# Retention and the product-key stage in one block: hoisted set-up, the second layer norm taken pair by pair, and the first similarities ahead of the later pairs' norms

## What is computed

```python
def _layer_norm(x): return (x - mean(x)) / sqrt(var(x) + 1e-5)
q = (x @ Wq_pk).reshape(b, n, P, HEADS, DIM_KEY).transpose(2, 0, 1, 3, 4)
sim = einsum('pbnhd,pkhd->pbnhk', q, pk_keys)
scores, idx = top_k(sim, 16)
score = scores[0][..., :, None] + scores[1][..., None, :]
final_scores, pk_idx = top_k(score.reshape(..., 256), 16)
```

## Time and profile before

| | |
|---|---|
| median of 3 runs | 2008.14 us (2007.32 to 2009.21) |
| the profiled execution | 2008.43 us |
| its span, first to last instruction | 2006.6 us |
| mean granted PE clock | 0.973 of full |
| PE busy | 1901.6 us, 95% of the span |
| DVE, ACT, POOL busy | 81%, 73%, 65% |
| token mixer | until 192.9 us |
| retention | 192.9 to 236.7 us |
| product-key stage ahead of its loop | 237.2 to about 278 us |
| loop of 64 items and the end | from about 278 us |

### The profile page before, as it was taken

The page is one execution under the profiler, slowest core; times in us unless marked ns, Lnnn a source line. Parts: engine busy times, 40 slices in busy tenths (PEclk is TensorE's granted clock), DMA queues, the critical chain, the costliest instruction groups (busy, mean ns, idle before and its releaser), DMA issues.

```text
span 2006.6 us, 43782 instructions
## 1 busy us (share of the span) xinstructions
PE 1901.6 (95%) x11398; PEld 1489.8 (74%) x11398; DVE 1627.7 (81%) x4843; ACT 1470.3 (73%) x2979; POOL 1313.5 (65%) x1568
## 2 busy tenths in 40 slices
PE   5985759999999999999999999999999999999997
PEld 3973547777777777777777777777777777777776
DVE  3654668888888888888888888888888888888886
ACT  2662357787877777877777778787778787777785
POOL 1210147777777777777777777777777777777774
PEclk9997769999999999999999999999999999999998
DMA  3000110002000010002000100010000100020001
GB/s 100 1 0 0 56 59 17 17 17 63 21 20 20 20 62 17 17 16 63 20 20 20 59 18 17 20 62 21 20 20 20 59 16 17 20 62 20 20 18 27
DMA packets 118151, 58.04 MB, mean 29 GB/s; under 512 B 109712, under 2 KB 116048, under 8 KB 116813
## 3 DMA queue, kind: packets, MB, share of 16 engines
q1 hardware_dynamic: 115298, 56.75, 10.4%
q10 hardware_dynamic: 2795, 0.70, 0.2%
HBM read 24.55 MB, written 0.70 MB: 13 GB/s over the span
## 4 chain that ended last, share of the span: by engine, by line
PE 84%; issue 1%; DVE 1%; ACT 1%; SPq 0%; POOL 0%; DMA 0%; ACTq 0%; DVEq 0%; POOLq 0%
PE ps L1016 29%; PE ps L1024 16%; PE ps L1007 15%; PE ps L1028 8%; PE ps L1066 5%; PE ps L1084 4%; PE ps L1001 2%; PE ps L1076 2%; PE ps L1051 2%; PE ps L1038 1%; PE ps L1044 1%; PE ps L1067 0%; SPq L959 0%; ACT k_W L1187 0%; DVE k_W L1475 0%
## 5 line engine op out<-in xcount | busy, mean ns | idle before, releaser
L1475 DVE SCALAR_TENSOR_TENSOR k_W<-ps,k_W 128x688 f32<-128x688 f32 x1028 | 893.9, 870 | 236.0 <-ACT k_W L1187 208.8
L1361 POOL TENSOR_TENSOR k_W_low<-k_W,k_W_high 128x688 fp32r<-128x688 f32 x513 | 851.3, 1660 | 336.5 <-ACT k_W_high L1192 336.5
L1187 ACT ACTIVATE k_W<-ps 128x688 f32<-128x688 f32 x1029 | 766.0, 745 | 376.7 <-PE ps L1007 357.1
L1016 PE MATMUL ps<-k_W,k_tab 128*128 128x344 f32 x2048 | 676.6, 453 | 0.0
L1007 PE MATMUL ps<-k_X,k_sel 128*128 128x344 f16 x2058 | 472.6, 311 | 25.6 <-DMA k_X<-k_spl 13.3
L1016 PEld LDWEIGHTS ps<-k_W,k_tab 128*128 128x128 f32 x2048 | 366.4, 190 | 127.3 <-issue 0.5
L1192 ACT ACTIVATE k_W_high<-k_W 128x688 fp32r<-128x688 f32 x513 | 395.8, 772 | 0.0
L1024 PE MATMUL ps<-k_W_high,k_tab_high 128*128 128x344 f32 x1024 | 386.0, 379 | 0.0
L1024 PE MATMUL ps<-k_W_high,k_tab_low 128*128 128x344 f32 x1024 | 324.9, 320 | 0.0
L1007 PEld LDWEIGHTS ps<-k_X,k_sel 128*128 128x128 f16 x2058 | 176.5, 99 | 196.9 <-issue 96.0
L1028 PE MATMUL ps<-k_W_low,k_tab_high 128*128 128x344 f32 x1024 | 244.4, 320 | 0.0
(11 more groups left out here) (227 smaller groups left out, 2355.7 us busy)
## 6 DMA issues: line engine op xcount, KB each, us to landing
k_tab<-in_tables SPq DMA_DIRECT2D x9, 2048.0 KB, 7.2
k_X<-k_spl SPq DMA_TRANSPOSE x390, 2.4
k_xs<-x2T SPq DMA_DIRECT2D x33, 172.0 KB, 2.1
k_qT<-k_qs SPq DMA_DIRECT2D x33, 86.0 KB, 2.1
cst<-in_consts SPq DMA_DIRECT2D x1, 1024.0 KB, 18.8
wts<-in_weights SPq DMA_DIRECT2D x1, 896.0 KB, 13.0
cst<-in_consts SPq DMA_DIRECT2D x1, 874.5 KB, 16.5
xr<-in_xrows SPq DMA_DIRECT2D x1, 750.0 KB
```

The source lines that it names most:

```text
L1016: mm = mm_(sums, tab[:, slot, at + k, :], W[:, d % RING, k, :], start=(d == 0 and k == 0), stop=(d == NDC - 1 and k == 1))
L1187: A(W[:, d % RING, :, :], ps[:, 2 * (d % 2):2 * (d % 2) + 2, 0:LOUT], ACT.Exp).then_inc(e_done, 1)
L1361: G.tensor_tensor(W_low[:, q % SPLIT_RING, :, :], W[:, d % RING, :, :], W_high[:, q % SPLIT_RING, :, :].bitcast(F32), ALU.subtract).then_i ...
L1475: V.scalar_tensor_tensor(W[:, d % RING, :, :], ps[:, 2 * (d % 2):2 * (d % 2) + 2, 0:LOUT], 0.0, W[:, d % RING, :, :], ALU.is_ge, ALU.mult) ...
```

## The change

One block `retention_and_keys` takes the place of the two blocks. In the order of the diff:

- The load of the key weights, the clearing of `wf`, the sixteen matmuls that form it and ACT's four copies of it move into `token_mixer`: the load last in SP's list, the clearing behind DVE's first `memset`s, the matmuls behind PE's last one, the copies behind ACT's last activation. The three casts go to POOL, behind its attention work.
- At the start of the joint block SP issues head 0's table and `wos`; DVE clears four buffers, POOL five. The retention's work buffers are laid into buffers that the loop uses later (`W`, the second table slot, `y`), and `P` and `PT` of the loop into the constants' tile, where cosines, sines, decay and `sel` lay. The retention scores use four PSUM banks in place of six, tiles 1 and 2 of the tokens in one.
- ACT rounds head 0's table behind the retention's value copies, and POOL forms its low part there, in place of DVE.
- The second layer norm is taken pair by pair: pair 0 between the mixes, the similarities of item 0 before `mix(3)`, the later pairs beside the first selection.
- PE waits for the even transposes ahead of the first log weights and for the odd ones only ahead of the fifth tile. The transposes of `hT` come after the last norm's logarithm. PSUM bank 5 is cleared by DVE after they are copied.

```diff
-                layer_norm(1, ret_done, 1)
+                retention_scores(0)
+                retention_scores(1)
+                mix(0)
+                retention_scores(2)
+                second_mean(0)
+                mix(1)
+                second_variance(0)
+                retention_scores(3)
+                mix(2)
...
-                pe.wait_ge(s_load, 32)
...
+                pe.wait_ge(ln_done, NPAIR + 1)
                 similarities(0, 0, 0)
...
+                mix(3)
+                for p in range(1, NPAIR):
+                    second_mean(p)
+                    second_variance(p)
+                pe.wait_ge(log_done, 2 * NPAIR)
                 for t, (t0, m) in enumerate(TT):
                     for p in range(NPAIR):
-                        mm = tr_(ps[0:m, (0, 1, 4)[t], 128 * p:128 * p + 128], hT[:, p, t0:t0 + m], eye)
+                        mm = tr_(ps[0:m, YBANK[t], 128 * p:128 * p + 128], hT[:, p, t0:t0 + m], eye)
                     mm.then_inc(y_mm0, 1)
...
                 similarities(1, 1, 0)
                 pe.wait_ge(x_even, 48)
-                pe.wait_ge(x_odd, 48)
                 for d in range(LEAD):
                     if d >= 2:
                         pe.wait_ge(w_done, d - 1)
+                    if d == 4:
+                        pe.wait_ge(x_odd, 48)
                     log_weights(0, 0, d)
```

```diff
+                for pair in range(NPAIR):
+                    for half in range(2):
+                        table_high(0, 1, pair, half)
+                squares(1, 0)
+                logarithm(1, 0)
+                deviation(1, 0)
+                act.wait_ge(zeroed, 9)
+                copy_similarities(0)
+                squares(1, 1)
+                logarithm(1, 1)
+                deviation(1, 1)
+                squares(1, 2)
+                high_part(0)
+                candidate_weights(0)
+                logarithm(1, 2)
+                deviation(1, 2)
+                squares(1, 3)
+                logarithm(1, 3)
+                deviation(1, 3)
```

```diff
+                decay(0)
+                decay(1)
+                add(0)
+                centred(1, 0)
+                decay(2)
+                add(1)
+                normed(1, 0)
+                decay(3)
+                add(2)
...
                 halves(0)
+                add(3)
+                centred(1, 1)
                 sums_max(0, False)
                 sums_drop(0)
                 sums_max(0, True)
                 threshold(0)
+                normed(1, 1)
+                centred(1, 2)
                 chosen(0)
+                normed(1, 2)
+                centred(1, 3)
+                normed(1, 3)
+                dve.wait_ge(y_ready0, NT)
+                V.memset(ps[:, 5, :], 0.0).then_inc(bank_zeroed, 1)
                 softmax_sum(0)
                 for d in range(LEAD - 1):
                     weights(0, d)
-                dve.wait_ge(tab_high_ready, 8)
-                for pair in range(NPAIR):
-                    for half in range(2):
-                        V.tensor_tensor(part_of(tab_low, 0, pair, half), rows_of(0, pair, half),
...
                 halves(1)
```

More of the change, by code:

```diff
@@ L385, in _ @@
                 nc.tensor.matmul(ps[:, 2, 0:NPAIR], weight("o2"), o2[:, :], start=True, stop=True).then_inc(tau_mm, 1)
+                pe.wait_ge(s_load, 16)
+                for k in range(2):
+                    for h in range(H):
+                        mm = nc.tensor.matmul(ps[0:64, k, 64 * h:64 * h + 64], pkw_sb[:, k, h, 0:64], pkw_sb[:, k, h, 64:128], start=True, stop=True)
+                    mm.then_inc(wf_mm, 1)
             @block.scalar
@@ L916, in score_area, with sim_bank @@
             return ((4 + pj, 0), (4 + pj, 128), (MID1, 0))[t]
+        def sim_bank(n):
+            return 5 if isinstance(n, int) and n == 0 else MID0
         def rounds(eng, body):
@@ new lines, in second_variance @@
+                def second_variance(p):
+                    pe.wait_ge(sqr_done, NPAIR + p + 1)
+                    if p == 1:
+                        pe.wait_ge(sim_ready, 1)
+                    if p > 1:
+                        pe.wait_ge(log_done, NPAIR + p)
+                    nc.tensor.matmul(ps[:, 5, 0:LOUT], const("mean"), sqr[:, p, :], start=True, stop=True).then_inc(var_mm, 1)
+                for w in range(2):
+                    for p in range(NPAIR):
+                        pe.wait_ge(ln_done, p + 1)
+                        if w == 1:
+                            pe.wait_ge(log_done, NPAIR)
+                        nc.tensor.matmul(ps[:, 4 * w + p, 0:LOUT], weight(("rq", "rk")[w]), x2T[:, p, :],
+                                         start=True, stop=True).then_inc(raw_mm, 1)
@@ new lines, in retention_scores @@
+                def retention_scores(p):
+                    pe.wait_ge(rot_ready, NPAIR + p + 1)
+                    if p == 0:
+                        pe.wait_ge(v_ready, NT)
+                        pe.wait_ge(sin_done, 2 * NPAIR)
+                    for t, (t0, n) in enumerate(TT):
+                        if p > 0 and t < 2:
+                            pe.wait_ge(dec_ready, 2 * NT * (p - 1) + (2, 6)[t])
+                        for b2 in range(2):
+                            rows = slice(64 * b2, 64 * b2 + 64)
+                            mm = nc.tensor.matmul(ps[0:n, 2 * b2 + SBANK[t], SCOL[t]:SCOL[t] + LOUT - t0], rqk[rows, 1, p, t0:t0 + n],
+                                                  rqk[rows, 0, p, t0:LOUT], start=True, stop=True)
+                            if t != 1:
+                                mm.then_inc(score_mm, 1)
@@ new lines, in mix @@
+                def mix(p):
+                    if p >= 2:
+                        pe.wait_ge(ret_done, p - 1)
+                    for t, (t0, n) in enumerate(TT):
+                        pe.wait_ge(dec_ready, 2 * NT * p + 2 * t + 2)
+                        for b2 in range(2):
+                            mm = nc.tensor.matmul(ps[64 * b2:64 * b2 + 64, 6 + p % 2, t0:LOUT],
+                                                  rv[0:n, t, 128 * p + 64 * b2:128 * p + 64 * b2 + 64],
+                                                  dec[p % 2][0:n, b2, DCOL[t]:DCOL[t] + LOUT - t0], start=(t == 0), stop=(t == NT - 1))
+                    mm.then_inc(ret_mm, 1)
```

372 lines of the change are left out of this document (153 added, 219 removed).

## The result

The changed kernel takes **1989.91 us** (median of 4, 1988.36 to 1991.51) against 2008.68 us (2007.32 to 2009.28), a ratio of 0.9906 [0.9894, 0.9918]: 18.8 us less, where 16.6 were forecast. It lies in the range; the path was right and several terms were mis-sized. The profiled execution took 1989.92 us and its span is 18.5 us shorter than before. One execution of this study, of the kernel in "The later norms ahead of the first selection", took 4258.93 us instead of 1995; it is left out of the medians and ratios, and nothing here explains it.

What follows compares the result with a forecast made beforehand. PE bounds the loop, a single thread of waits the stretch ahead of it. Log weights 13.9 us earlier plus 2.7 for the low part gave 16.6 us: 2008.4 − 16.6 = 1991.8, predicted 1992, range 1988.5 to 1997.5.

Steps and rivals of the forecast that it cites:

- the path: Ahead of the loop: selection, low part, transposes, log weights, fifth weights as a single thread; 1990.5 to 1994 us, chance 0.55.
- Port term: Table rounding ahead of the first retention scores: one DVE addition slowed beside POOL's low parts, +0.33 us, ends 0 and 0.8.
- its dearer reading: Exclusive lock between DVE and POOL held for a whole instruction: cost a whole POOL pass rather than 0.33 us.
- Pair 0's chain: Pair 0's second norm between the mixes, then first similarities: halves(0) starts at 231.4 instead of 244.6, 13.2 us earlier.
- late start: Set-up moved into the mixer, ahead of the retention's first mean: cost taken as 0, with upper ends for load and clears.
- The landing, 249.0: Third DMA transpose landing before the first log weights: 242.8 + 3 × 1.29 + 2.35 = 249.0, earlier than PE's 250.9.
- The low part off DVE, 2.7: Table's low part leaves DVE ahead of the fifth weights in item 0: all 2.7 us count.
- The loop, 0: Loop after its entry: PE bounds it and its body is unchanged, so no change; wrong if over 2 us.
- rival D: Inner loop turns begin to cost 1.9 us like outer ones, 24 of them, 46 us: 2037 us; chance 0.04.
- rival A: Later norms ahead of log weights late behind ACT's rounding and candidate weights: 3.9 us lost, 1996 us; chance 0.20.
- the half-clock durations: Later norms, transposes and item 1's similarities on PE taken at 1.2 GHz, about 1.5 us from matmul start to reader.

Runs made afterwards that it cites:

- The later norms ahead of the first selection: Changed kernel with the second norms of all pairs, in PSUM banks of their own, ahead of item 0's similarities and selection: 1994.66 us, ratio 0.9928 to the kernel before.
- norms abreast: Changed kernel with separate PSUM banks for each pair's mean and variance, pairs 2 and 3 normed step by step together: 1985.05 us, ratio 0.9877 to the kernel before.
- the repeat: The changed kernel measured and profiled once more with no edit: 1987.54 us, ratio 0.9902 to the kernel before.
- padded runs: Kernel before with 16 or 32 unread one-column activations added on ACT behind its last mixer activation: 2003.43 us with 16, 2008.72 us with 32.

## Why the prediction was right, and where it was off

- **The path held.** Selection, low part, transposes and log weights came in the order forecast, each within 0.8 us, and the log weights stood behind item 1's similarities, not behind a DMA. The order of selection and norms is the change's main part: 9.3 us (norms first against norms abreast).
- **Port term, 0.33.** It measured 0.6 (22.81 against 22.23 us), of which the rows show 0.50. The addition lost 0.50 to the POOL pass that had started 0.08 before it and had some 0.68 left (6.09 us for eight passes is 0.76 each). The lock told of in the Trainium skill's "SBUF — State Buffer", section "SBUF: two separate sides", agrees as far as the addition waited for most of what was left of the pass; its dearer reading, a whole pass, did not come, and the last addition, with POOL's passes around it, took its usual 0.52.
- **Pair 0's chain.** From the first scores to `halves(0)` the forecast had 15.6 us and the changed kernel took 13.9. The run with the low part on DVE took 15.7. What differs is how long PE's clock was low there: 3.4 us of 1.2 GHz in the one, 6.8 in the other and in the kernel before. This is not chance: the low-clock stretch behind the first scores lasts 3.4 us in all nine profiled executions with POOL's low parts in that place and 6.8 in all five without. The scores to `halves(0)` take 13.9 to 14.5 us in the eight of the nine that keep the order of selection and norms, and 15.7 in both of the changed kernels without. So the move that costs 0.6 to 0.8 us ahead of the scores gives 1.7 to 1.8 behind them, 0.9 to 1.2 net, and the forecast had only the cost; by which step POOL's work shortens the low stretch is not shown. The windows over these seven microseconds, changed kernel first, then the other (columns as in the earlier trace rows):

```profile
217.00:224.00 7.00, 6.92 (x49) 5.15 (x50) 4.64 (x14) 0.28 (x1) 4.30 (x6) 0.76 0.01 2
```

```profile
217.20:224.20 7.00, 6.50 (x38) 4.35 (x39) 4.28 (x14) 0.75 (x3) 0.00 (x0) 0.57 0.01 2
```

  PE issued 49 matmuls in place of 38. The forecast's durations mixed rows at both clocks without saying which would hold; that part of the error, about 1.7 us, is the clock's, and by the runs it came with the moved low part. With the late start (0.9) and the port (0.3 more) it leaves 0.6.
- **The landing, 249.0.** It stands at 247.5 (242.36 + 5.1). I had read 262.29 in the earlier trace rows as the end of the sixth issue; from 255.82 on, at 1.29 each, it is the end of the fifth, and the 2.35 behind it hold the sixth's issue and landing. The third landing is therefore one issue earlier than 3 × 1.29 + 2.35. As the norm chain ended at 250.55, this cost nothing in the sum, but it made the chain look less late than it was: 1.9 us forecast between the two, 3.1 measured. An answer to "what would it give to take the norms abreast" would have been too small by that.
- **The low part off DVE, 2.7.** 2.6 by the run that undid it, from log weights to the fifth `weights`; 3.2 from the traces before and after. With the two effects ahead of the selection the move is worth 3.7 us.
- **The loop, 0.** This step failed: "the loop follows as it is, since PE bounds it". It lost 0.4 us in its first item (the shift fell from 17.4 to 17.0; what took them is not shown, and the repeat, at the full clock there, took 1.7 less for the same stretch), 0.4 in each of two early items (the 2nd and the 10th took 26.6 instead of 26.15), and gained 0.7, 1.0 and 0.7 at the three outer turns: about 1.1 in all to the last instruction, which with 17.4 is the measured 18.5. That is inside the 2 us that the prediction had named as its limit; in the repeat the shift grew by 3.5 us between the fifth and the last `weights`, which is outside it. I had read the gap of 1.9 us at the turn and only asked whether it might get more frequent (rival D), not whether its length depends on where ACT's instructions lie. The runs with activations added to the kernel before show that it does.
- **The norms late (rival A)** did not come: the variances' hand-overs took what was forecast (246.66 for the start of the transposes, 246.6 in the forecast). **D** came with the opposite sign.
- **The clock.** The windows of the changed kernel, while PE was in the norms and behind them:

```profile
235.00:251.50 16.50, 11.68 (x32) 7.07 (x32) 7.10 (x27) 7.88 (x18) 5.60 (x13) 0.50 0.16 38
252.00:255.00 3.00, 0.93 (x4) 0.23 (x4) 2.15 (x3) 2.07 (x4) 0.00 (x0) 1.00 0.78 300
```

  The clock stayed at 0.50 through the transposes and the similarities, in which PE was busy without a pause from 246.66, and was at 1.00 from 251.8 on, but for 3.4 us each at 255.2 and 262.0. The Trainium skill's "TensorE: Matmul & The Clock Gate", section "What's actually happening", by which activity releases the throttle, is borne out, but the release came after the work that would have gained by it: the half-clock durations were the right choice.

## What to carry to other kernels

Where several engines pass one thread along ahead of a loop, put what has the longest latency behind it (here a selection, a rounding and DMA transposes) ahead of work that only has to be done by the same point, and then look at what ends last anew: it was the norms, and giving each pair its own PSUM bank took off another 3 us. Read an idle stretch put down to "issue" at a loop's turn on every engine: ACT's changed with 16 instructions added far ahead of the loop, and stretches of up to 2.65 us cost nothing here, those of 3.27 and more 0.6 to 0.75 us each. Check a move's price past the place where it is paid: POOL's passes cost 0.6 us ahead of the scores and came with 1.8 us less behind them. And compare events inside an execution: the same kernel's profiled spans differ by 4.7 us, and of the 5.0 us by which 16 instructions that do nothing seemed to shorten one, 3.3 were an earlier start and a shorter end.

## What the runs showed that I had not expected

- Three outer turns of an unchanged loop body became 0.7 to 1.0 us shorter each, and adding 16 activations to the kernel before did nearly the same (0.6 to 0.9): ACT's stretch went from 3.33 to 2.49 us. The number of the `instruction` queue's packets doesn't explain it: it is 45 in the page of the kernel before and in both of its padded runs, long turns or short, and also 45 in the changed kernel with 16 activations, whose turns are as short as with 30. What fills ACT's stretch stays open.
- The mixer's end lies between 190.8 and 194.5 us from one execution or edit to the next, with stretches at 1.2 GHz that begin at other times.
- Six DMA transposes issued one after the other take 7.72 us to issue, and the last has landed about 1.2 us after its issue ended.
- A DVE pass with both operands in SBUF waits for a running POOL pass: two norms took 1.80 us beside POOL and 0.94 without.
